# One multiplication per token tile for the linear context of the first attention, and its context read over all 128 rows

## The reference, cut to what matters

```python
def causal_linear_attn(q, k, v):            # BUCKET = 64, n = 512, e = 16
    q = jax.nn.softmax(q, axis=-1)
    k = jax.nn.elu(k) + 1.0
    bq, bk, bv = (z.reshape(b, h, u, BUCKET, e) for z in (q, k, v))
    k_cum = jnp.cumsum(bk.sum(axis=-2), axis=-2)
    ctx = jnp.einsum('bhund,bhune->bhude', bk, bv)
    ctx = jnp.cumsum(ctx, axis=2)
    ctx = ctx / (k_cum[..., None] + 1e-06)
    ctx = jnp.pad(ctx, ((0, 0), (0, 0), (1, 0), (0, 0), (0, 0)))[:, :, :-1]
    out = jnp.einsum('bhund,bhude->bhune', bq, ctx)
```

## Time and profile before

| | |
|---|---|
| time, median of 3 runs | 2844.01 us (2837.87 to 2846.75) |
| span of the profiled execution | 2831.8 us |
| median time less that span | 12.2 us |
| PE busy | 2659.5 us (94%) |
| ACT, DVE, POOL busy | 1858.8 us (66%), 1939.5 us (68%), 1051.8 us (37%) |
| chain that ended last | PE 73%, DVE 11%, ACT 7% |

### The profile page before, as it was taken

How to read it: one execution, slowest core, us unless ns; L and a number is a source line. 1 busy time by engine, 2 the same in 40 slices (tenths; PEclk the granted TensorE clock), 3 DMA queues, 4 the chain that set the end, 5 groups by cost and what they waited for, 6 DMA issues and landing times.

```text
span 2831.8 us, 63348 instructions
## 1 busy us (share of the span) xinstructions
PE 2659.5 (94%) x24036; PEld 1812.7 (64%) x24036; DVE 1939.5 (68%) x5616; ACT 1858.8 (66%) x4392; POOL 1051.8 (37%) x876
## 2 busy tenths in 40 slices
PE   8999999999999998899999998998898998998998
PEld 5666656548888885588888885455455563553554
DVE  5555646488788786788888886774675326764774
ACT  5666766626676673478787876776776515875875
POOL 2323323313333330355555552553454013552551
PEclk8999999999999998999999999999999999999999
DMA  1010000000000001000000002210210002111210
GB/s 56 1 43 1 13 1 9 5 9 2 3 2 2 2 2 50 30 2 2 2 2 2 2 2 92 62 45 7 61 49 20 24 1 69 47 30 30 49 42 16
DMA packets 35280, 63.13 MB, mean 22 GB/s; under 512 B 11526, under 2 KB 15654, under 8 KB 33830
## 3 DMA queue, kind: packets, MB, share of 16 engines
q1 hardware_dynamic: 34982, 59.07, 7.5%
HBM read 23.48 MB, written 1.15 MB: 9 GB/s over the span
## 4 chain that ended last, share of the span: by engine, by line
PE 73%; DVE 11%; ACT 7%; issue 3%; SPq 2%; POOL 1%; DMA 1%; DVEq 0%; ACTq 0%; POOLq 0%
PE bank L804 63%; PE bank L1033 5%; PE bank L1153 3%; SPq L770 2%; PE bank L880 1%; ACT low L1364 1%; DVE low L1708 1%; DVE low L1686 1%; ACT work L1400 1%; ACT work L1303 1%; DVE halves L1701 1%; DMA work<-work 1%; DVE work L1588 1%; ACT squared L1275 1%; ACT bank L1279 1%
## 5 line engine op out<-in xcount | busy, mean ns | idle before, releaser
L1271 ACT ACTIVATE low<-bank 128x512 f32<-128x512 f32 (+3 forms) x512 | 427.8, 946 | 0.0
L804 PE MATMUL bank<-table_keys,halves 128*128 128x512 f32 (+3 forms) x1536 | 418.0, 380 | 1.1 <-ACT low L1364 1.0
L804 PE MATMUL bank<-work 128*64 128x128 f32 (+6 forms) x4480 | 364.2, 290 | 39.7 <-DVE work L1795 20.7
L804 PEld LDWEIGHTS bank<-work 128*64 128x64 f32 (+3 forms) x4480 | 265.0, 144 | 211.5 <-issue 147.5
L1364 ACT ACTIVATE low<-bank,low 128x512 f32<-128x512 f32 (+23 forms) x384 | 227.2, 592 | 248.9 <-DVE low L1708 245.4
L1708 DVE TENSOR_REDUCE low<-bank 128x1 f32<-128x512 f32 (+22 forms) x512 | 286.4, 569 | 96.2 <-PE bank L804 91.3
L1898 POOL TENSOR_TENSOR halves<-squared,const 128x512 fp32r<-128x512 f32 x128 | 137.0, 1070 | 510.7 <-PE bank L804 510.7
L1271 ACT ACTIVATE work<-bank 128x512 f32<-128x512 f32 (+4 forms) x389 | 199.5, 538 | 151.2 <-PE bank L804 76.9
L804 PEld LDWEIGHTS bank<-table_keys,halves 128*128 128x128 f32 x1536 | 243.6, 190 | 47.6 <-issue 13.3
L1400 ACT ACTIVATE work<-work 128x192 f32<-128x192 f32 (+1 forms) x512 | 218.7, 431 | 38.2 <-DVE work L1788 38.2
L1947 POOL TENSOR_TENSOR work<-work 128x768 f32<-128x768 f32 x128 | 187.7, 1466 | 135.2 <-DVE work L1799 135.2
(11 more groups left out here) (201 smaller groups left out, 5707.3 us busy)
## 6 DMA issues: line engine op xcount, KB each, us to landing
work<-work SPq DMA_DIRECT2D x512, 64.0 KB, 2.0
slot<-in_wW SPq DMA_DIRECT2D x4, 1605.5 KB, 6.7
slot<-in_wA SPq DMA_DIRECT2D x4, 837.0 KB, 6.4
table_low<-embv_padded SPq DMA_DIRECT2D x2, 1536.0 KB, 6.3
table<-in_dft SPq DMA_DIRECT2D x1, 3072.0 KB, 11.8
slot<-in_wE SPq DMA_DIRECT2D x2, 584.0 KB, 3.7
const<-in_const SPq DMA_DIRECT2D x1, 1094.5 KB, 5.2
squared<-in_x SPq DMA_DIRECT2D x4, 256.0 KB, 6.2
```

Source lines behind the costliest of these rows:

```text
L804: return pe.matmul(o, l, r, start=start, stop=stop)
L1271: return act.activation(dst, src, ACT.Identity)
```

## The change

```diff
@@ a_context on PE
-                for u in range(1, NB_A):
-                    dst = o[0:64, (u - 1) * 65:u * 65]
-                    for a in range(u // 2):
-                        last = mm(dst, KF[:, a, :], TM[:, b, a, 192:257], start=(a == 0), stop=(a == u // 2 - 1 and u % 2 == 0))
-                    if u % 2:
-                        a = u // 2
-                        last = mm(dst, KF[0:64, a, :], TM[0:64, b, a, 192:257], start=(a == 0), stop=True)
+                ctx_of = o[0:64, 0:(NB_A - 1) * 65].rearrange("p (u f) -> p u f", u=NB_A - 1)
+                for a in range(NT - 1):
+                    later = NB_A - 2 * (a + 1)
+                    mm(ctx_of[:, 2 * a + 1:, :], KF[:, a, :], bc(TM[:, b, a, 192:257].unsqueeze(1), [P, later, 65]),
+                       start=(a == 0), stop=False)
+                for a in range(NT):
+                    last = mm(ctx_of[:, 2 * a, :], KF[0:64, a, :], TM[0:64, b, a, 192:257], start=False, stop=(a == NT - 1))
                 last.then_inc(tile_full, 1)
@@ window_values on PE
                 for u in (2 * s.w, 2 * s.w + 1):
-                    mm(o[:, u * BUCKET:(u + 1) * BUCKET], CN[0:64, b, u].rearrange("p h a d -> p (h a d)"),
-                       QT[0:64, b, u * BUCKET:(u + 1) * BUCKET], start=(u == 2 * s.w), stop=False)
+                    mm(o[:, u * BUCKET:(u + 1) * BUCKET], CN[:, b, u].rearrange("p h a d -> p (h a d)"),
+                       QT[:, b, u * BUCKET:(u + 1) * BUCKET], start=(u == 2 * s.w), stop=False)
@@ a_context on DVE
                 if s.n == 0:
-                    link(dve.memset(CN[0:64], 0.0))
+                    link(dve.memset(CN, 0.0))
+                    link(dve.memset(QT[64:P], 0.0))
```

## The result

| | before | changed |
|---|---|---|
| median | 2844.01 us (2837.87 to 2846.75) | 2821.53 us (2819.50 to 2822.93) |
| ratio | | 0.9929 (95%: 0.991 to 0.9948) |
| span of the profiled execution | 2831.8 us | 2821.2 us |

A fourth run of the kernel before was slow, at 3706.33 us, and is left out of its median and of the ratio. The time fell by 0.7%: the ratio gives 20 us of 2844, the medians differ by 22.5. The forecast was 2826.3 with a range of 2818 to 2836.

A forecast was written before the change was run, and what follows sets the result against it. PE was taken to bound these layers nearly everywhere. Context -15.0, `CN` multiplications -3.6 and memset +0.9 sum to -17.7 us: span 2831.8 to 2814.1, plus 12.2 around it, 2826.3 us; range 2818 to 2836.

The forecast's parts named there:

- The price of a change: On PE, one change of the weights' shape costs 0.09 us ahead plus 0.05 for the late second record, 0.14 us.
- The context run: First transpose to first `CN` record: 2.45 us instead of 3.38, 0.93 less a lane at full clock; 15.0 us over 16 lanes.
- Rival 1: Context's repeated moving operand streams slower; at twice the record time 22.4 us are added, giving 2848.7 us; chance 0.06.
- Rival 2: Half tiles in a row in the context don't hide their weight loads; 4.7 us missing, giving 2831.0 us; chance 0.06.
- `CN` over 128 rows: Windows behind a 512-column record lose the change ahead of `CN`: 0.14 us a window, 3.6 us in all.
- Rival 4: Change of shape goes by columns or pair, not rows, so 128-row `CN` gains nothing; 3.6 us missing, 2829.9; chance 0.07.
- Rival 3: Path goes over to DVE and ACT; context saving given back in half the lanes, 7.5 us missing, 2833.8; chance 0.12.
- An inner lane: From one context to the next without a clock fall, 1.07 us less; squared-norm wait grows from 0.57 to about 0.85.
- The memsets: At the chain's DVE memset, the wider one stays at 1.78 us; the new one adds 0.93 us once, on the path.
- The clock: PE's clock halves behind longer waits; falls may come, go or change length, no direction seen, +-3.4 us in the range.
- Rival 5: Falls of PE's clock go away with shorter runs ahead of them: 3 to 7 us less, about 2821 us; chance 0.07.
- The 12.2 us around the span: Time outside the profiled span, added to the forecast span of 2814.1 us to give 2826.3 us.

The follow-up runs named there:

- interleaving: Changed kernel with the half tiles placed ahead of each whole tile, eight changes of shape instead of three: 2832.91 us, ratio 0.9988.
- the plain transposes: Changed kernel with the four transposes of q ahead of the context made as ordinary multiplications by the identity: one time 2830.98 us, inner lanes 21.38 us.
- the changed kernel with the work put back: Changed kernel plus four unread 57-column multiplications (eight records) at the end of each context run: 2839.54 us, ratio 1.0006.

## Why the prediction was right, and where it was not

The range held, the sign and the mechanism (changes of shape go away) are shown. That the point forecast of 17.7 us came within 3 us of the first measured gain (20 us by the ratio) is in part luck: it hides two errors that partly cancel, too much gain by work (point 2) and none by the clock (point 7).

1. *The price of a change*, 0.09 + 0.05 us, holds: interleaving put five of them back and cost 5 x 0.14 us.
2. *The context run*, 0.93 us: it is 0.78. The step that failed is "transposes, 4 x 0.11 = 0.44, with no change behind them, since they too have 128*64 weights". The trace writes the same shape for both, but the change is there, and the plain transposes move it. It was there to be seen in the trace: PE goes from 128*128 weights into L846 without the 0.09 us (0.12 from start to start, as between the records ahead), so that the transposes behave as those do. So three changes are left and not two: five of the eight go, not six. That one term is 16 x 0.15 = 2.4 us of the sum.
3. *The moving operand that reads the same columns again* runs at full rate: 0.33 us for 390 columns, the lower bound. Rival 1 is out. *Half tiles in a row* follow each other at 0.058 us: 85.77 to 86.27 are 0.50 us, seven of them (0.41) and the change out (0.09). Rival 2 is out: 65 columns at the rate of the 256-column records (0.216 us) would take 0.055 us, so next to nothing is left for a load that isn't overlapped. The Trainium skill's rule ("TensorE: Matmul & The Clock Gate", Part 3, The mechanism) that a weight load overlaps running multiplications only when the row group differs does not agree with these rows; the same section also has an exception for loads into the background weight buffer.
4. *`CN` over 128 rows*: a window gains 0.20 us, not 0.14 (the second record comes 0.056 behind the first instead of 0.16; I had 0.11, the spacing of the next two). What reaches the time is 0.18 us in an inner lane, one window of four, since three of them are followed by waits in the same lane or stand behind a context. I had counted one of four too. Rival 4 is out. Rival 3 (the saving given back in half of the lanes) is out too, as every inner lane is shorter by 0.96.
5. *An inner lane*: forecast 1.07 us less, measured 0.96, which is the 0.15 too much of point 2 less the 0.04 too little of point 4. The wait at the squared norm grew to 0.71 us and not 0.85. A second wait ahead of it took the rest: PE's norm multiplication (`inner,const`) starts 1.20 us behind the first record of the group ahead of it (94.83 to 96.03), before 1.03 (75.06 to 76.09). It now waits for DVE's sum of the residual, which ends at 95.97:

```profile
95.23 0.74 DVE L1509 SCALAR_TENSOR_TENSOR inner<-bank,slot,inner 128x512 f32<-128x512 f32 x1
```

6. *The memsets*: 0.93 us forecast for the new one; its step of the chain is 0.92 us, with 0.26 between the two, 1.2 in all. They lie on the path, as said: with both at the head of the program PE stands still 2.9 us less in the first lane.
7. *The clock*: "I see no direction in it and put +-3.4 us into the range." This failed. The kernel before has a fall behind the 1.9 us wait in lane 0 of layers 2, 3 and 4 in every trace, nine of nine, at 2.6 us each. The changed kernel has one short fall in six such lanes. That is 7.8 us of gain with one sign, less the 0.5 us of that short fall (20.81 against 20.3 us behind the same MLP stretch). Summed by lanes from the first traces, the first block is 22.8 us shorter: 4 x 2 x 0.96 = 7.7 from the inner lanes, 3 x 1.2 + 1.1 = 4.7 from the last lanes and the MLP behind them, 3.0 + 3.5 + 3.5 = 10.0 from lane 0 of layers 2 to 4, and 0.3 from the first lane. With 2.6 us a fall, some 7 us of the 10.0 are clock and some 15 to 16 of the 22.8 are work. So by work alone the forecast gain was some 2 us too large. Rival 5 happened beside it, and I had called it 7% likely; that the falls left because the work ahead of them is shorter is not shown.
8. *The 12.2 us around the span* (launch and end) are wrong: of the runs whose span is on record, time less span is 1.7 to 1.9 us. The other 10 are the distance from a short execution to a typical one. The sum was not hurt, as the same number went off and on.

What stays open is why the falls leave. Less work is not it alone (the changed kernel with the work put back has none), and the long wait of PE alone is not it either: it is 1.92 us before and 2.11 us after. With more work the fall of the kernel before grew. What decides whether a fall comes was not found.

## What to carry to other kernels

Order small multiplications by the shape of their weights: on this path each change between them cost 0.14 us, as much as 2.4 records of 65 columns. Grouping sixteen of them gave nine tenths of what seven longer ones gave. Filling up to the neighbour's shape with zeros paid here where that neighbour had the full 128*128. Before a gain of under 1% is put down to an edit, compare stretches at equal clock in the two traces: here a third of the first block's gain was clock, and seven other microseconds of work came with 22 to 28 us.

## What the runs showed of the hardware

- A transpose with 64 columns of weights stands in the trace as 128*64, follows records with 128*128 weights at once and is followed by ordinary 128*64 ones with the 0.09 us of a change.
- A moving operand with a step of zero streams as fast as a plain one (0.33 us for 390 fp32 columns, 0.22 for 260).
- A run of 64*64 or 128*64 records with new weights for each goes on at 0.058 us for 65 fp32 columns; a change of rows or columns of the weights adds 0.09 us ahead of the first such record and 0.05 ahead of the second.
- The same 164 PE records of a lane took 23.71 us with a fall of the clock and 21.11 without.
- A stretch of some 34 us at half clock (mean 0.54 over 618 to 652) can come in code that no edit touched; it came in five of fourteen traces, and 224 records took 34.0 us in it instead of 21.6.
